# An interaction tower on one core: the order of its 64 units per chunk written out by hand, two of four row sums moved from VectorE to ScalarE, the dense pieces at other units, transposes two units ahead instead of four

## The reference

```python
e = jnp.stack([tbl_f[ids[:, f]] for f in range(32)], axis=1)        # 1024 x 32 x 64
p, q = e[:, ROW_IDX], e[:, COL_IDX]                                 # 496 pairs i < j
z = jnp.einsum('bne,hne,bnh->bn', p, kernel, q)                     # kernel: 64 x 496 x 64
h = jnp.concatenate([z, dense_ctx], axis=1)                         # 1024 x 512
h = jnp.maximum(h @ W_top1 + b_top1, 0.0)                           # 512 x 512
h = jnp.maximum(h @ W_top2 + b_top2, 0.0)                           # 512 x 256
y = h @ W_top3                                                      # 256 x 1
```

## Time and profile before

| what | value |
|---|---|
| median of three runs | 456.8 us (454.54 to 457.21) |
| profiled execution: its own time | 454.52 us |
| profiled execution: span | 452.7 us, mean granted TensorE clock 0.981 |
| PE matmul busy | 396.2 us (88% of the span) |
| PE weight loads busy | 222.8 us (49%) |
| DVE busy | 347.8 us (77%) |
| ACT busy | 323.2 us (71%) |
| POOL busy | 242.5 us (54%) |
| the chain of waits that ended last | PE 57%, ACT 21%, DVE 7%, POOL 7%, issue 6%, DMA 2% |

### The profile page before, as it was taken

How to read it: one execution, slowest core, us unless ns; L and a number is a source line. 1 busy time by engine, 2 the same in 40 slices (tenths; PEclk the granted TensorE clock), 3 DMA queues, 4 the chain that set the end, 5 groups by cost and what they waited for, 6 DMA issues and landing times.

```text
span 452.7 us, 9545 instructions
## 1 busy us (share of the span) xinstructions
PE 396.2 (88%) x2912; PEld 222.8 (49%) x2912; DVE 347.8 (77%) x381; ACT 323.2 (71%) x2594; POOL 242.5 (54%) x260
## 2 busy tenths in 40 slices
PE   0224799999979999999989999999969999999957
PEld 0113344545545564655545555555545556555536
DVE  1123599999985798799987789799969789899901
ACT  1000479987993799667994799658986798768961
POOL 5777777777777777777777777777400000000000
PEclk9999899999998999999989999999999999999988
DMA  5776981111111111111111111111000000000000
GB/s 124 166 162 155 225 221 29 28 26 28 28 27 28 30 27 28 27 28 29 28 30 29 28 27 29 26 28 29 18 1 3 0 2 2 1 2 1 1 1 0
DMA packets 13635, 19.28 MB, mean 43 GB/s; under 512 B 5584, under 2 KB 6928, under 8 KB 13584
## 3 DMA queue, kind: packets, MB, share of 16 engines
q1 hardware_dynamic: 5392, 10.27, 9.5%
q0 software_dynamic: 8192, 8.40, 8.3%
HBM read 18.65 MB, written 0.00 MB: 41 GB/s over the span
## 4 chain that ended last, share of the span: by engine, by line
PE 57%; ACT 21%; DVE 7%; POOL 7%; issue 6%; DMA 2%; DVEq 0%
ACT rows_prod L367 20%; PE bil L554 20%; PE bil L539 13%; PE z_ps L574 11%; POOL gathered L347 7%; PE side_ps L599 5%; DVE rows_prod L440 2%; PE side_ps L604 2%; DVE prod L449 2%; PE bil L522 1%; DMA gathered<-in_tbl,ids_sb 1%; PE z_ps L589 1%; PE bil L635 1%; PE bil L659 1%; DVE prod L456 1%
## 5 line engine op out<-in xcount | busy, mean ns | idle before, releaser
L367 ACT ACTIVATE rows_prod<-rows_prod 128x64 f32<-128x64 f32 x1280 | 305.9, 242 | 99.3 <-DVE rows_prod L440 99.0
L347 POOL DMA_INDIRECT gathered<-in_tbl,ids_sb x256 | 242.3, 947 | 80.4 <-issue 77.5
L367 ACT ACTIVATION_READ_ACCUMULATOR rows_prod<-rows_prod 128x1 f32 x1280 | 240.9, 188 | 0.0
L554 PE MATMUL bil<-emb,k_sb 64*128 64x256 f32 x1280 | 172.3, 398 | 8.7 <-DVE emb L428 6.9
L449 DVE TENSOR_TENSOR prod<-bil,emb 128x1024 f32<-128x1024 f32 x128 | 153.9, 1215 | 17.7 <-PE bil L554 17.5
L554 PEld LDWEIGHTS bil<-emb,k_sb 64*128 64x128 f32 x1280 | 121.7, 194 | 81.0 <-issue 42.1
L440 DVE TENSOR_TENSOR rows_prod<-bil,gathered 128x1024 f32<-128x1024 f32 x96 | 116.3, 1215 | 18.6 <-PE bil L539 18.6
L539 PE MATMUL bil<-k_sb,emb 64*128 64x512 f32 x384 | 102.8, 617 | 0.9 <-DVE rows_prod L440 0.8
L574 PE MATMUL z_ps<-prod,sel_sb 128*32 128x512 f32 x576 | 85.2, 605 | 0.0
L539 PEld LDWEIGHTS bil<-k_sb,emb 64*128 64x128 f32 x384 | 33.1, 186 | 32.5 <-issue 14.1
L428 DVE COPY emb<-bil 128x512 f32<-128x512 f32 x32 | 21.8, 680 | 34.3 <-PE bil L522 34.3
(11 more groups left out here) (31 smaller groups left out, 83.7 us busy)
## 6 DMA issues: line engine op xcount, KB each, us to landing
k_sb<-in_k_blocks SPq DMA_DIRECT2D x24, 256.0 KB, 4.9
gathered<-in_tbl,ids_sb POOLq DMA_INDIRECT x256, 2.4
k_sb<-in_k_blocks SPq DMA_DIRECT2D x8, 192.0 KB, 6.1
inner<-in_dense_rows SPq DMA_DIRECT2D x64, 1.0 KB
w_sb<-in_w SPq DMA_DIRECT2D x1, 1024.0 KB
k_sb<-in_k_blocks SPq DMA_DIRECT2D x8, 64.0 KB, 4.6
w_sb<-in_w SPq DMA_DIRECT2D x1, 512.0 KB
ids_sb<-in_ids SPq DMA_DIRECT2D x1, 128.0 KB, 2.1
```

The lines of the kernel that those rows point to most:

```text
L347: pool.indirect_dma_start(gathered[:, q % 2, t, field * EMBED:(field + 1) * EMBED], None, tables[field], bass.IndirectOffsetOnAxis(ap=ids_ ...
L367: last = act.activation(row, row, ACT.Copy, accum_out=z_rows[:, t, half, col:col + 1])
L554: last = pe.matmul(out[:, s, i * CHUNK:(i + 1) * CHUNK], k_sb[rows, n, :], e[rows, j, :], start=True, stop=True)
```

## The change

```diff
-BATCH_PAIRS = [0, 0, 1, 2, 2, 2, 2, 3]
+ORDER = ["", "ff", "bbbb", "bfbbfb", "fffbbfff", "bfbbfffbff", "bbffbbffbfbf", "fffbffbbfbffff"]
...
-        couples = [(x, m) for x in range(0, k - 1, 2) for m in range(2)][:BATCH_PAIRS[k]]
+        couples = [(x, m) for x in range(0, k - 1, 2) for m in range(2)][:ORDER[k].count("b") // CT]
         firsts = [own[1 + m * k + x] for x, m in couples]
-        batch = [("batch", n, t) for n in firsts for t in range(CT)]
-        fields = [("fields", n, 0) for n in own[1:] if n not in firsts and n - 1 not in firsts]
-
-        count = len(batch) + len(fields)
-        places = [x * count // len(batch) for x in range(len(batch))]
-        units += [batch.pop(0) if x in places else fields.pop(0) for x in range(count)]
+        batch = iter([("batch", n, t) for n in firsts for t in range(CT)])
+        fields = iter([("fields", n, 0) for n in own[1:] if n not in firsts and n - 1 not in firsts])
+        units += [next(batch) if x == "b" else next(fields) for x in ORDER[k]]
...
-SUM_UNITS = [10, 20, 30, 40]
+SUM_UNITS = [8, 52]
...
-    return max(first - 4, q * NU + FIRST_OF[k - 1] + 1) if k else max(first - 4, 0)
+    return max(first - 2, q * NU + FIRST_OF[k - 1] + 1) if k else max(first - 2, 0)
...
-PIECE_UNITS = [10, 20, 30, 40]
+PIECE_UNITS = [9, 14, 32, 56]
```

## The result

The changed kernel takes 434.5 us (median of 4 runs, 433.44 to 435.18), the kernel before beside it 455.7 (4 runs, 453.94 to 457.21): a ratio of 0.953 (0.949 to 0.958), 21.2 us less. The forecast was 439.5 us in a range of 434 to 449. The profiled execution took 433.44 us with a span of 431.6.

The account below looks back on a forecast made before the run. A full period was taken as PE's work plus 2.0 us plus ACT's lateness. 131.1 + 97.5 + 96.7 + 95.8 + 14.2 = 435.3 us of span, 17.4 less: 456.8 - 17.4 = 439.4, predicted 439.5, range 434 to 449.

Parts of the forecast that it names:

- First chunk: Up to the first turn: ACT starts at 46.0, makes 22 sums without a gap, turn at 131.1, 5.4 us gained.
- Transposes two ahead: PE's transposes in full periods: bank pair waits for the copy either way, cost 0; outer bound 12 us a chunk.
- The reduce moved into the wait: At each of three chunk boundaries, a reduce runs under PE's wait for quad 1's copy: 1.0 us gained, between 0 and 1.2.
- ACT in the full periods: Full periods: with 22 sums ACT is ready 95.8 us after a turn, and decides only the fourth turn.
- PE in the full periods: Full periods: PE, its work unchanged in number, is ready after 96.7 us and decides by 0.9.
- Second turn: Period before the second turn: 96.7 plus half of 1.6 for the low clock, 97.5 us, 3.8 less.
- The wait before l1b: PE before dense piece l1b, until ACT has written l1a: 19.8 against 19.0 us, just covered; 1 us if uncovered.
- Tail: After the last turn: 0 to 3.0 us less than 15.7 from full clock; middle taken, 1.5, giving 14.2.
- (a): Rival, whole kernel: only ACT's 8.2 us of lateness goes, first chunk and boundaries stay, 448.6 us; chance 0.11.
- (b): Rival, full periods: ACT becomes the bound, ready after 99.5 us if 5 us of idling stay, 449.4 us; chance 0.08.
- (c): Rival: slower, the ring of four buffers stalls DVE in bursts and ACT starves; periods of 107.3, 473 us; chance 0.04.
- (d): Rival: no shift, ACT's two extra sums use up what earlier places give, turns stay, 455 to 458 us; chance 0.05.

Follow-up runs that it names:

- e7: The changed kernel with one row sum on VectorE (after unit 52) and 23 on ScalarE: 442.1 us, ratio 0.970.
- e8: The changed kernel with quad 1's transposes before unit 63 of the chunk before instead of before unit 65, after the first chunk: 432.1 us, ratio 0.948.
- e11: The changed kernel with the dense pieces back at units 10, 20, 30 and 40: 435.2 us, ratio 0.956.
- e10: The changed kernel with the transposes four units ahead again instead of two: 447.7 us, ratio 0.984.
- e3: The kernel before with the transposes two units ahead instead of four, alone: 455.8 us, ratio 1.002.
- e4: The kernel before with the dense pieces at units 9, 14, 32 and 56 instead of 10, 20, 30 and 40, alone: 460.8 us, ratio 1.012.
- e6: The changed kernel with the last quad's four batch units at 59 to 62 instead of 53, 56, 57 and 59: 466.5 us, ratio 1.023.
- e1: The kernel before with the new order of units alone: 450.2 us, ratio 0.989.
- e9: The kernel before with the new order and VectorE row sums after units 8 and 52, pieces and transposes as before: 444.3 us, ratio 0.975.
- e5: The changed kernel with VectorE row sums after units 8, 20, 30 and 52 instead of 8 and 52: 435.4 us, ratio 0.956.

## Why the prediction was right

The forecast's mechanism held and its result was 5 us too high. Step by step:

- **First chunk**, 5.4 us forecast, 5.9 measured. ACT started at 45.95 (46.0 forecast), had no gap, and the turn began at 130.62 (131.1). The forecast waits of the ring, 3.7 us at units 42, 45 and 47, were 0.41 at unit 47 alone. PE was nevertheless ready only at about 130.3, as forecast (130.5), so some 3 us of gain on DVE that the forecast counted didn't come; that these two errors cancel is luck, and they were not decisive only because ACT was. e7, e8 and e11 confirm it: their first turns follow ACT's first sum by the length of its sums.
- **Transposes two ahead**, 0 in the periods. As a term of the sum against the kernel before it was right: neither kernel has a wait for a multiply in its full periods. Its reason was not. I argued that the bank is used either way, three uses later; e10 shows that where the transposes stand is worth 2.4 us a period in this order, and e3 that the same edit costs as much in the old order. The sum came out only because the new order and the new places fit.
- **The reduce moved into the wait**, 1.0 forecast. It was half of that. The reduce is PE's work in either place, so the gain is what the wait shrinks by: from 2.02 to 1.54, 0.48 us, where the prediction's sign was a wait of about 1.0. DVE's copy came some 0.5 us later than forecast, within the 0 to 1.2 that the prediction left open.
- **ACT in the full periods**, ready 95.8 us after a turn. It was ready at 96.7 - 2.7 = 94.0, 1.8 earlier. Its busy time in all was 350.7 us (354 forecast), DVE's 338.0 (338). The last period, which I let ACT decide at 95.8, was PE's: 94.8.
- **PE in the full periods**, 96.7 forecast, 96.72 measured. The number is exact by luck: of the 1.0 us less than 97.7, 0.48 is the boundary's, and the other half is PE's busy time, 95.16 instead of 95.70 for the same matmuls, which the forecast held unchanged. The last period shows the same: 94.90 instead of 95.50. The wait before l1b, "just covered", does not appear.
- **Second turn**, 97.5 forecast with half of the slow-clock spell; the clock was 1.00 and the period 96.75.
- **Tail**, 14.2 forecast, as the middle of 12.7 to 15.7. It was 12.7, the clock staying at 1.00 in the window that answers to the one where it had been 0.50. Here the throttled state being the default that activity releases (the Trainium skill, TensorE: Matmul & The Clock Gate, What's actually happening) was the better guide than my middle: all runs with PE waiting 3.2 us or more before the last turn have tails of 15.0 to 15.7 (before, e3, e4, e6), all with 1.3 or less 12.7 or 12.8.

The measured span is 3.7 below the forecast's 435.3: 0.5 in the first chunk, 0.75 in the second turn's clock, 1.0 in the last period, 1.5 in the tail. No step failed in its direction; the largest mis-sized term is the tail, the reduce's term was twice too large, and the loss of hidden waits was not in the sum. A further 1.2 us of the 4.9 in the median come from the 2.3 us by which I let the median stand above the profiled execution; it stands 1.1 above.

Of the rivals, (a) is refuted by the first chunk and by the period of 96.7, below the 97.7 that removing waits alone leaves. (b) needs ACT late, which had 2.7 us in hand at the second and at the third turn; e7 shows how near that is: with one sum more, 3.83 us, ACT is late again before the last turn, by 1.26. The mechanism of (c) exists: DVE waits 1.0 us a period in e1 and 2.68 + 0.87 in e7. In the change it is 0.41 in the first chunk and none later. (d) is refuted by every turn.

The prediction also weighed a page's caution that matmul busy time doesn't show how near TensorE is to its limit (the Trainium skill, Perfetto Trace Analysis, Identifying the Most-Contended Engine), and set it aside. The traces agree with the page: the same matmuls take 95.70 us of busy time in the kernel before, 95.16 in the change and 96.3 in e9. In e9 that is 1.1 us of the period beside the 0.6 in its three brackets, so there PE's busy time does hold waits for DVE; in the kernel before it is some 0.5.

What stays open: where in the kernel before the 0.5 us of hidden waits lie, and how much of e6's 8 us a period is its late copy and how much its clock. The new order together with the new transposes and the old four row sums was not run, so the sums' share of the 21 us is known only as 5.9 beside the old transposes (e1 to e9) and about 1 to 2 in the change, for two sums fewer (e5).

## What to carry to other kernels

When an engine at 70 to 80% of the span still decides where a phase ends, look at when its last work arrives, and move that work earlier before moving it elsewhere; then follow its queue from the first item, because start plus count times length gave this kernel's first turn within 0.5 us. In a shared ring of buffers a short use (here transposes) counts as a full one, so put work of the producer that uses no buffer of that ring beside it. Waits for it can be missing from the idle time, so compare busy times for the same work too. Edits to one hand-written order must be judged together: alone these four gave +3 us, together -21.

## What the runs showed of the hardware

- Sixteen activations of 128x64 with an accumulator output, each followed by the accumulator's read, take 3.83 us one behind the other, 0.24 a pair, although the groups by line give 245 ns for the one and 191 for the other: the two overlap almost wholly.

```profile
L365 ACT ACTIVATE rows_prod<-rows_prod 128x64 f32<-128x64 f32 x1408 | 336.1, 245 | 56.0 <-DVE rows_prod L438 56.0
L365 ACT ACTIVATION_READ_ACCUMULATOR rows_prod<-rows_prod 128x1 f32 x1408 | 269.3, 191 | 0.0
```

- The gather of quad 3, the same instructions in every kernel here, let PE go on between 47.47 and 48.97 us. Where ACT's first sum stands behind it, it moves that sum: 51.11 us with the gather at 47.66 (before), 52.78 with the gather at 48.97 (e4). It doesn't account for the spread of the times: four runs of e9, with the sum behind the gather, lie within 0.4 us, ten of e3, with it ahead, within 3.6.
- A wait of 2.77 us before a turn (e6, 347.16) left the turn at 1.08 us, one of 2.69 before another (137.91) was followed by a turn of 1.94 us, with a granted clock of 0.58 from 138 to 142: the length of one wait doesn't tell the clock.
